# Self attention with rounded plain scores, interleaved routing chains and a reordered activation engine

## What is computed

```python
nx = _layernorm(x, ln1_w, ln1_b)            # 32 batches, 112 rows, 256 features
q, k, v = jnp.split(nx @ Wqkv + bqkv, 3, axis=-1)   # 16 heads of 16
scores = jnp.einsum('bqhd,bkhd->bhqk', q, k) / jnp.sqrt(jnp.float32(HEAD_DIM))
scores = jnp.where(causal, scores, jnp.finfo(scores.dtype).min)
attn = jax.nn.softmax(scores, axis=-1)
x = x + jnp.einsum('bhqk,bkhd->bqhd', attn, v).reshape(B, S, D) @ Wo + bo
nx2 = _layernorm(x, ln2_w, ln2_b)
topk_vals, topk_idx = jax.lax.top_k(nx2 @ gate_W, TOP_K)   # 2 of 8 experts
```

## Time and profile before

| | us |
|---|---|
| median of three runs | 2081.35 (2074.27 to 2083.16) |
| the profiled execution, its own time | 2102.62 |
| its span (first to last instruction) | 2100.8 |
| PE busy over the span | 1989.4 (95%) |
| DVE, ACT, POOL busy | 1356.7, 1066.4, 895.2 |
| self attention, first moments to routing table | from about 521 to 894 |

### The profile page before, as it was taken

How to read it: one execution, slowest core, us unless ns; L and a number is a source line. 1 busy time by engine, 2 the same in 40 slices (tenths; PEclk the granted TensorE clock), 3 DMA queues, 4 the chain that set the end, 5 groups by cost and what they waited for, 6 DMA issues and landing times.

```text
span 2100.8 us, 60752 instructions
## 1 busy us (share of the span) xinstructions
PE 1989.4 (95%) x21151; PEld 1659.6 (79%) x21152; DVE 1356.7 (65%) x3358; ACT 1066.4 (51%) x2466; POOL 895.2 (43%) x1522
## 2 busy tenths in 40 slices
PE   7999999997989999799999999979999999999995
PEld 5888888885767777589999999857777877777784
DVE  6777777774668787643333333247878778787775
ACT  3555555553556665322332233346666666666662
POOL 4545454542366666500000000156666566666651
PEclk9999999998999999799999999989999999999997
DMA  8232323220620000111111111310101111110100
GB/s 221 84 109 82 109 82 108 83 85 2 237 87 22 22 22 22 50 58 37 37 35 35 39 35 35 97 33 20 42 28 38 31 37 32 30 39 28 39 19 10
DMA packets 98074, 118.76 MB, mean 57 GB/s; under 512 B 9442, under 2 KB 90466, under 8 KB 97890
## 3 DMA queue, kind: packets, MB, share of 16 engines
q1 hardware_dynamic: 91874, 103.32, 16.1%
q0 software_dynamic: 6144, 14.69, 2.4%
HBM read 67.26 MB, written 50.72 MB: 56 GB/s over the span
## 4 chain that ended last, share of the span: by engine, by line
PE 59%; issue 26%; POOL 5%; ACT 3%; DVE 3%; another core or an unknown queue 1%; POOLq 1%; DMA 0%; ACTq 0%; DVEq 0%; SPq 0%
PE ps_proj L258 19%; PE ps_quad L578 5%; PE ps_quad L136 4%; PE ps_out L158 4%; PE ps_turned L147 4%; PE ps_out L586 3%; PE ps_proj L1818 3%; PE ps_proj L1797 3%; PE ps_proj L662 2%; PE ps_turned L564 2%; PE ps_out L1169 1%; PE ps_out L669 1%; PE ps_proj L1823 1%; ACT a_probsT L413 1%; PE ps_quad L564 1%
## 5 line engine op out<-in xcount | busy, mean ns | idle before, releaser
L1307 ACT ACTIVATE e_act_T<-ps_quad,fc_b 128x128 f32<-128x128 f32 x504 | 137.2, 384 | 314.9 <-PE ps_quad L1388 314.9
L1388 PEld LDWEIGHTS ps_quad<-e_xT,e_w_now 128*128 128x128 f32 x2016 | 236.3, 193 | 7.6 <-DVE e_xT L1347 4.6
L1388 PE MATMUL ps_quad<-e_xT,e_w_now 128*128 128x128 f32 x2016 | 237.2, 276 | 3.7 <-DVE e_xT L1347 3.7
L1403 PE MATMUL ps_out<-w,e_act_T 128*128 x1008 | 228.1, 379 | 0.8 <-DVE e_y L1355 0.8
L413 ACT ACTIVATE a_probsT<-ps_quad 125x1792 f32<-125x1792 f32 x96 | 160.0, 1666 | 100.5 <-PE ps_quad L578 100.5
L1403 PEld LDWEIGHTS ps_out<-w,e_act_T 128*128 128x128 f32 x1008 | 186.6, 190 | 24.0 <-issue 1.2
L1344 DVE COPY e_w_now<-w 128x2048 f32 (+1 forms) x63 | 77.3, 1227 | 190.6 <-PE ps_quad L1388 189.4
L1536 POOL MEMSET c_cT<- 128x2 f32 x2 | 0.1, 102 | 463.7 <-DMA c_wk<-in_L_xattn_Wk 463.7
L1532 POOL TENSOR_TENSOR c_kL<-c_kT,c_kH 128x376 fp32r<-128x376 f32 x128 | 126.4, 988 | 155.6 <-ACT c_kH L1601 154.9
L1596 ACT ACTIVATE c_kT<-ps_proj 128x376 f32<-128x376 f32 x128 | 62.0, 484 | 176.7 <-PE ps_proj L258 175.6
L178 DVE TENSOR_SCALAR c_probs<-c_probs,c_recip 112x375 f32<-112x375 f32 x256 | 148.3, 620 | 4.6
(11 more groups left out here) (314 smaller groups left out, 5345.9 us busy)
## 6 DMA issues: line engine op xcount, KB each, us to landing
slots<-a_zeros SPq DMA_DIRECT2D x60, 512.0 KB, 4.9
a_cT<-in_ctx_t SPq DMA_DIRECT2D x32, 375.0 KB, 3.6
c_cT<-in_ctx_t SPq DMA_DIRECT2D x32, 375.0 KB, 3.2
w<-in_fc_t SPq DMA_DIRECT2D x2, 4096.0 KB, 19.2
w<-in_fc_t SPq DMA_DIRECT2D x8, 1024.0 KB
e_xg<-slots SPq DMA_DIRECT2D x63, 128.0 KB, 2.0
slots<-e_y SPq DMA_DIRECT2D x63, 128.0 KB, 1.7
out<-c_fo SPq DMA_DIRECT2D x32, 112.0 KB, 1.9
```

Of the source, the lines that this page charges most:

```text
L1307: last = act.activation(act_T[par][:, c * TILE:(c + 1) * TILE], hidden[par][:, c // 4, (c % 4) * TILE:(c % 4 + 1) * TILE], ACT.Gelu, bias= ...
L1388: last = pe.matmul(hidden[par][:, c // 4, (c % 4) * TILE:(c % 4 + 1) * TILE], w1_now[:, k, c * 128:(c + 1) * 128], xT[par][:, k, :], start ...
L1403: last = pe.matmul(y_ps[:, 0:D], act_T[1 - par][:, c * TILE:(c + 1) * TILE], w2[:, bass.ds(e, 1), c, :].rearrange("p a d -> p (a d)"), sta ...
```

## The change

The plain scores, which serve only for the row maximum, are made from rounded operands. ACT writes a rounded q (`q_high`, unmasked) from the same PSUM as q; POOL writes a rounded k with two masks (`k_high`, one for each head of a pair), so that one matmul of 224 columns makes two heads. The exact scores are as before. ACT's k copy moves from the head of the next step into the step where the product is made; n2 moves ahead of it and nn behind it. The `oT2` copy keeps its place behind the q copy, and the new `q_high` copy stands behind `oT2`. The V product on PE waits for `q_high` (`q_rounded`) in place of q (`q_whole`). On DVE the two routing chains `place` and `choose`, each a row of small dependent instructions, are cut into pieces that alternate with each other and with reciprocal and `on`. Four semaphores of the last sublayer are allocated earlier in its function; their use is the same.

```diff
@@ POOL, behind the masked copy of q
+                        pool.wait_ge(k_ready, nxt + 1)
+                        wait(pool, plain_mm, nxt)
+                        pool.tensor_tensor(k_high[:, :, :, :], kT[1 - par][:, :, :].unsqueeze(2).to_broadcast([128, 2, 2, T]),
+                                           mem["qmask"][:, :].unsqueeze(1).unsqueeze(3).to_broadcast([128, 2, 2, T]), ALU.mult)\
+                            .then_inc(k_rounded, 1)
@@ ACT
-                    if exists(b):
-                        act.wait_ge(k_mm, b + 1)
-                        (k copy of b, at the head of the step)
...
-                    if exists(ahead):
-                        (nn)
                     if exists(b - 2):
                         (n2)
+                    if exists(nxt):
+                        act.wait_ge(k_mm, nxt + 1)
+                        (k copy of nxt)
+                    if exists(ahead):
+                        (nn)
                     (q copy)
                     (oT2 copy)
+                    if exists(nxt):
+                        wait(act, plain_mm, nxt)
+                        for t in range(2):
+                            last = act.activation(q_high[:, t, :], pb[:, t * T:(t + 1) * T], ACT.Identity, bias=bqk[:, t:t + 1])
+                        last.then_inc(q_rounded, 1)
@@ DVE step, behind the maximum
                     if exists(b - 4):
-                        place(b - 4, par)
+                        rank_sum(b - 4)
+                    if exists(b - 3):
+                        largest(b - 3, 1 - par)
+                    if exists(b - 4):
+                        rank_slot(b - 4)
                     (reciprocal)
+                    if exists(b - 3):
+                        largest_index(b - 3)
                     (on)
+                    if exists(b - 4):
+                        place(b - 4, par)
                     if exists(b - 3):
-                        choose(b - 3, 1 - par)
+                        index_copy(b - 3)
+                    if exists(b - 4):
+                        placed(b - 4)
+                    if exists(b - 3):
+                        pick_both(b - 3)
+                        choose(b - 3)
@@ PE, plain_scores
-                            for e in range(2):
-                                for r in range(4):
-                                    at = (2 * t + e) * T
-                                    last = pe.matmul(quad[0:T, r, at:at + T], qT[par][group(r), t, e, :], kT[par][group(r), t, :],
-                                                     start=False, stop=True, skip_group_check=True)
+                            for r in range(4):
+                                at = 2 * t * T
+                                last = pe.matmul(quad[0:T, r, at:at + 2 * T], q_high[group(r), t, :],
+                                                 k_high[group(r), t, :, :].rearrange("p e t -> p (e t)"),
+                                                 start=False, stop=True, skip_group_check=True)
@@ PE step
-                        pe.wait_ge(q_ready, b + 1)
-                        pe.wait_ge(k_ready, b + 1)
+                        pe.wait_ge(q_rounded, b + 1)
+                        pe.wait_ge(k_rounded, b + 1)
                         plain_scores()
...
                         pe.wait_ge(shift_ready, b + 1)
+                        pe.wait_ge(q_ready, b + 1)
                         scores()
...
-                        pe.wait_ge(q_whole, nxt + 1)
+                        pe.wait_ge(q_rounded, nxt + 1)
                         (V product)
```

More of the change, by code:

```diff
@@ L723, in self_attention @@
         kT = [sb(f"kT{i}", [128, 2, T]) for i in range(2)]
+        q_high, k_high = sb("q_high", [128, 2, T], F32R), sb("k_high", [128, 2, 2, T], F32R)
         v = [sb(f"v{i}", [T, H, 32]) for i in range(2)]
@@ L747, in self_attention @@
         nT_mm, nT_ready = sem("nT_mm"), sem("nT_ready")
-        q_mm, q_whole, q_ready = sem("q_mm"), sem("q_whole"), sem("q_ready")
-        k_mm, k_ready = sem("k_mm"), sem("k_ready")
+        q_mm, q_whole, q_ready, q_rounded = sem("q_mm"), sem("q_whole"), sem("q_ready"), sem("q_rounded")
+        k_mm, k_ready, k_rounded = sem("k_mm"), sem("k_ready"), sem("k_rounded")
         v_mm, v_ready = sem("v_mm"), sem("v_ready")
@@ L871, in step @@
                     nxt, ahead = b + 1, b + 2
-                    if exists(b):
-                        act.wait_ge(k_mm, b + 1)
-                        for t in range(2):
-                            last = act.activation(kT[par][:, t, :], pa[:, t * T:(t + 1) * T], ACT.Identity,
-                                                  bias=bqk[:, 2 + t:3 + t])
-                        last.then_inc(k_ready, 1)
                     if exists(b - 1):
@@ L900, in step @@
                         act.activation(shift[:, :], shift_out, ACT.Copy).then_inc(shift_ready, 1)
-                    if exists(ahead):
-                        act.wait_ge(rates_ready, ahead + 1)
-                        wait(act, nT_mm, ahead)
-                        act.activation(nn[:, :], row(residual, ahead), ACT.Identity,
-                                       scale=row(rates, ahead)[:, 1:2], bias=row(shifts, ahead)[:, 1:2]).then_inc(nn_ready, 1)
                     if exists(b - 2):
@@ L911, in step @@
                                        scale=o_rate[par][:, :], bias=o_shift[par][:, :]).then_inc(n2_ready, 1)
+                    if exists(nxt):
+                        act.wait_ge(k_mm, nxt + 1)
+                        for t in range(2):
+                            last = act.activation(kT[1 - par][:, t, :], pa[:, t * T:(t + 1) * T], ACT.Identity,
+                                                  bias=bqk[:, 2 + t:3 + t])
+                        last.then_inc(k_ready, 1)
+                    if exists(ahead):
+                        act.wait_ge(rates_ready, ahead + 1)
+                        wait(act, nT_mm, ahead)
+                        act.activation(nn[:, :], row(residual, ahead), ACT.Identity,
+                                       scale=row(rates, ahead)[:, 1:2], bias=row(shifts, ahead)[:, 1:2]).then_inc(nn_ready, 1)
                     if exists(nxt):
@@ L979, in place, with pick_both, placed, choose @@
                     dve.tensor_tensor(earlier[:, :], earlier[:, :], chosen[:, :], ALU.add).then_inc(place_step, 1)
+                def pick_both(m):
+                    dve.wait_ge(choose_step, CHOOSE * m + 3)
+                    dve.tensor_tensor(pick[:, :, :], expert_no[0:T, :].unsqueeze(1).to_broadcast([T, TOP, NE]),
+                                      top_atf[:, :].unsqueeze(2).to_broadcast([T, TOP, NE]), ALU.is_equal).then_inc(choose_step, 1)
+                def placed(m):
                     dve.wait_ge(place_step, PLACE * m + 5)
                     dve.sem_inc(slot_ready, 1)
+                def choose(m):
+                    dve.wait_ge(choose_step, CHOOSE * m + 4)
+                    dve.tensor_tensor(chosen[:, :], pick[:, 0, :], pick[:, 1, :], ALU.add).then_inc(chosen_ready, 1)
                 def step(b, par):
@@ L1434, in cross_last @@
         index = [[sb(f"index{i}{s}", [T, 1], U32) for s in range(TOP)] for i in range(2)]
+        wk_in, wv_in, k_split, v_split = sem("wk_in"), sem("wv_in"), sem("k_split"), sem("v_split")
         ratio, denom = sb("ratio", [T, NB]), sb("denom", [T, NB])
```

36 lines of the change are left out of this document (20 added, 16 removed).

## The result

| | us |
|---|---|
| kernel before, median of 4 runs | 2082.26 (2074.27 to 2084.43) |
| changed kernel, median of 4 runs | 2103.85 (2101.27 to 2103.98) |
| ratio, 95% interval | 1.0099 [1.0085, 1.0113] |
| profiled execution of the changed kernel, its own time | 2103.98 (span 2102.2) |

Of one kernel further down (the changed kernel with exact plain scores) two of five executions fell into a slower state, at 2177.8 and 2185.9 us, and its time is the median of the other three.

The account below looks back on a forecast made before the run. PE was nearly full but not the pace; the path ran from DVE's maximum through PE and a late increment to ACT's `oT2`, then y. Loop +16 and ends +1 made +17 on 2081.35: 2098 us, range 2077 to 2112.

Parts of the forecast that it names:

- the hold: PE's increments to ACT held while POOL builds scatter descriptors: 0.50 us late in both steps, 2 x 0.50 a pair.
- ACT's and PE's new order: V waits for `q_high` behind `oT2`: steps of 10.49 and 10.91 us, pair 21.40 against 21.15, +0.25 a pair.
- Rival C: The scores' increment itself is caught, as in the long step: +31 + 1 us, 2113; chance 0.10.
- Carrying the +17 over to the median: Profiled execution 21 us above the median, taken as spread over all stages; +17 added to 2081.35 gives 2098.
- PE's saving worth nothing: Plain scores on PE: 0.45 to 0.75 us a step saved, counted 0, since PE then waits for DVE's maximum.
- POOL: `k_high` takes 0.94 to 1.14 us, hidden in POOL's 2.1 us a step of waiting for y.
- DVE and the scatter: Interleaved chains make `slot_ready` about 0.7 us later; scatter 0.1 to 0.35 later, in the short step 0 to 0.1.
- A: Rival: later scatter, L1152's increment no longer caught; pair 21.40, +4 us, 2086; chance 0.28, 0.10 more for one step.
- B: The forecast itself: increments 0.50 us late in both steps, pair 22.40, +17 us, 2098; chance 0.42.
- D: Rival: PE's freed time brings L1152 0.3 us or more earlier; steps 10.2, -9 us, 2072; chance 0.10.
- E: Rival: POOL is the bound, `k_high` and later scatter fill 1.5 of 2.1 us; no loss by itself, no chance given.
- The port: y on DVE shares SBUF interfaces with POOL's `k_high`; at half speed 12 us more, left out of the sum.

Follow-up runs that it names:

- the pair without sends: Both scatters left out of the kernel before (2078.78 us) and of the changed kernel with exact plain scores (2101.09 us).
- the order was mended: Changed kernel with the V product moved behind the output product on PE, sends kept: 2078.82 us beside a before of 2082.36, ratio 0.9985.

## Why the prediction was right, and where it was not

The forecast was +17 us, to 2098; measured were +21.6, to 2103.85, inside the range. But its two main terms were wrong in opposite directions, +3 for the order, where 17 was measured, and +13 for the hold, where there was none. The right total is luck.

- **ACT's and PE's new order.** The mechanism and its steps were right to some hundredths. From y to the turn of the maximum 3.92 and 4.34 were forecast, 3.83 and 4.33 measured (720.96 - 717.13, 731.90 - 727.57); 2.47 from there to the turn of `on`, as forecast (723.43 - 720.96); 0.91 from its end to V, measured 0.94 (724.78 - 723.84); 2.78 from V to y, measured 2.79. Steps of 10.49 and 10.91, measured 10.44 and 10.93.
- **The base it was held against.** Here is the step that failed. "A pair without any hold is 21.40, against 21.15 now" compares the new order without a hold with the old order that has one. Without it before's pair is 19.95 (9.90 + 10.05), measured with the sends left out. The order alone costs 21.37 - 19.95 = 1.42 a pair, not 0.25; times 12 pairs 17.0 us. The first three steps add 2.6, for which the forecast had 1 (9.04, 9.30 and 10.07 became 9.96, 10.30 and 10.74 in the pair without sends). Over all 31 intervals of y that pair differs by 21.1 us (303.9, 325.0), of 22.3 in the medians. A row that could have warned was at hand: 9.30 between two y's that have no scatter beside them.
- **The hold.** It was given 0.50 a step in the new order, 1.00 x 13 = +13 us. In the changed kernel's trace of the first comparison it is 0, and its timed runs take as long. The reading that an increment is held the more, the deeper it falls into the scatter is wrong: at the same depth of 1.12 to 1.14 us it was 1.66 late in before's trace, 0.95 in the changed kernel on one chip and not late (0.04) in the same kernel on another. Nor is the 0.50 of before's short step all lateness. Its row has no idle time: ACT came from the q copy. Without sends `oT2` starts 0.25 behind the row's end in that step as well (706.39 against 705.73 + 0.41, shown above). On a chip that does have late increments, the hold costs the changed kernel 35 us (2138.8 - 2103.9) and the kernel before 20 (2102.0 - 2082.4). The loss is then 36.8 us. Rival C, whose +32 was summed against a before with the hold, comes nearest to that, with the scores' own increment late, as it said; the clock's fall to its lower level was in no step of it.
- **Carrying the +17 over to the median.** "The difference is in all stages" was not read from a row. The changed kernel's two traces say otherwise: with late increments its 31 intervals of y sum to 359.0 us, without to 328.5, 30.6 less, and the two spans differ by 32.3 (2134.5, 2102.2). So nearly all of it lies in this stage. For the kernel before, of which no trace with prompt increments and its sends exists, this is inferred.
- **PE's saving worth nothing.** Right: the plain scores take 0.47 a step (0.3 to 0.6 given), and PE waits 0.45 and 0.97 for the maximum. With exact plain scores and nothing sent the steps are the same as in the changed kernel, 10.43 and 10.94.
- **POOL.** Right: `k_high` takes 0.93 to 0.94, the lower of the bounds, and POOL still waits 31.3 us for y, 1.3 a step.
- **DVE and the scatter.** 0 to 0.35 later was given; from the rank sum to the scatter are 2.06 and 2.26 us (731.59 to 733.65, 720.74 to 723.00) against 2.07. Worth nothing without late increments, as the chains put back showed. With them, interleaving alone gains 11.7 us in the kernel before. This was no part of the sum.
- **The rivals.** A (no hold any more) had right what the trace shows, though not for its reason, since the send lies as deep as before, and the wrong time, 2086, for the reason of the wrong base. B's hold was not there. C is about what a chip with late increments shows. D and E did not occur: no steady step is 10.2, and POOL is not the bound.
- **The port.** The 12 us more that the forecast gave for y at half speed, and left out of its sum, are not in the changed kernel (y takes 483 to 486 ns in all 24 steps from 599.2 to 845.3), since `k_high` ends 0.4 us before y there (727.15, y at 727.57). It came up when the order was mended, and not as half speed: y waited `k_high` out.

## What to carry to other kernels

When the profiled execution is longer than the timed runs of the same kernel, find the stage that has the difference before anything is summed, and take both sides of a comparison with or without it: a new order without a stall against an old one with it gives a small number that means nothing. In a chain that is walked, an operand that moves behind another engine's copies costs the copies and all that is queued behind the waiting instruction; here a product whose result nobody was short of stood in front of the one on which the step depended, and moving it behind is worth 25 us (2103.9 to 2078.8). After shortening a path, look for what it now runs into.

## What the runs showed of the hardware that I had not expected

- Increments of PE reach the others well behind the end of the matmul's row (1.66 us, 1.25 and 0.95 above) on two chips and in before's profiled execution, and 0.04 (ACT) and 0.07 to 0.08 us (DVE) behind it in the traces of two others and of the first comparison's changed kernel. They came only beside indirect DMAs that POOL issues (none in the four kernels without the sends). The kernel before loses 20 us to it, the changed one 35. What decides between the groups stays open (the chip and the moment changed together), and so does the path on which an increment is late. The Trainium skill, Perfetto Trace Analysis, Tensor Engine Instruction, lets an increment follow PSUM's acknowledgement; the rows at 713.42 and 723.84 agree (0.04 us), the row at 679.81 doesn't (0.95).
- A wait of PE of 1.66 us was followed by products at 1.77 and 1.91 us in place of 1.12 and 1.03, with a granted clock of 0.50 (683.0 to 684.5); after a wait of 0.75 us they took 1.12 and 1.03. A wait of 2.40 us at the first sends (590.25) was followed by 2.05 and 1.91, again at 0.50. A late increment thus costs more than its lateness.
- y, an instruction of DVE with two inputs in SBUF, makes next to no headway while POOL's product runs, and ends 0.29 to 0.30 us behind it (0.48 alone). The Trainium skill, SBUF — State Buffer, SBUF: two separate sides, says that the port pair that DVE and GpSimd share is "an exclusive lock, not a bandwidth split"; this case's rows agree, and what it costs is set by where the two meet: 0.51 and 0.75 us a step here, nothing in the steady steps of the changed kernel.
